# A block of feed-forward, attention and feed-forward on one core: maxima of the first half of tokens beside the first Q and K, ranking behind the next maxima, dot products behind the statistics

## The reference, cut to what matters

```python
# x: 8 samples x 1024 tokens x 512
def ffn(x):                       # capacity 0.75: the 768 tokens with the largest scores
    scores = x @ w_router
    top = top_k(scores, 768)
    return x with gelu(x[top] @ w_block) at the places top
def attn(x):                      # 16 heads of 32, latents of 64, causal
    Q = x @ Wq.T
    lk, lv = x @ Wk_down.T, x @ Wv_down.T
    q_lat = einsum('bthd,hdl->bthl', Q, q_to_latent)
    attn = softmax(causal(q_lat @ lk.T / 8))
    heads = einsum('bthl,hld->bthd', attn @ lv, v_up)
    return heads @ Wout.T
x = x + 0.5 * ffn(layernorm(x))   # first feed-forward, s = 0, f = 0
x = x + attn(layernorm(x))        # attention, s = 1
x = x + 0.5 * ffn(layernorm(x))   # second feed-forward, s = 2, f = 1
```

## Time and profile before

| | |
|---|---|
| median of 3 runs | 2528.2 us (2514.88 to 2531.42) |
| the profiled execution's own time | 2527.03 us |
| its span | 2525.3 us |
| PE busy | 2256.9 us, 89% |
| DVE busy | 1805.5 us, 71% |
| ACT busy | 1179.3 us, 47% |
| POOL busy | 396.6 us, 16% |
| mean granted clock of PE | 0.957 |

### The profile page before, as it was taken

The page is one execution under the profiler, slowest core; times in us unless marked ns, Lnnn a source line. Parts: engine busy times, 40 slices in busy tenths (PEclk is TensorE's granted clock), DMA queues, the critical chain, the costliest instruction groups (busy, mean ns, idle before and its releaser), DMA issues.

```text
span 2525.3 us, 53119 instructions
## 1 busy us (share of the span) xinstructions
PE 2256.9 (89%) x21504; PEld 1399.1 (55%) x21504; DVE 1805.5 (71%) x5077; ACT 1179.3 (47%) x2070; POOL 396.6 (16%) x510
## 2 busy tenths in 40 slices
PE   5769999899889998899998999989998899988976
PEld 4534477445664556644675446654476445664445
DVE  5658748887677766787667875788757787677726
ACT  3325643465424654356534564445543465424442
POOL 0101111112101121111211102111211112101121
PEclk9869999999998999999998999999999899998998
DMA  3200021100201002010111102210021100301000
GB/s 129 100 1 3 2 84 51 68 2 15 87 35 68 2 18 84 34 69 3 39 62 54 49 2 68 68 68 3 2 92 43 68 2 2 101 1 68 2 2 34
DMA packets 69601, 106.42 MB, mean 42 GB/s; under 512 B 2544, under 2 KB 32752, under 8 KB 67312
## 3 DMA queue, kind: packets, MB, share of 16 engines
q1 hardware_dynamic: 69360, 103.03, 12.0%
HBM read 64.75 MB, written 37.75 MB: 41 GB/s over the span
## 4 chain that ended last, share of the span: by engine, by line
PE 66%; DVE 14%; issue 11%; ACT 7%; POOL 2%; DMA 0%; DVEq 0%; POOLq 0%; ACTq 0%
PE psum L726 22%; PE psum L739 18%; PE psum L839 9%; PE psum L846 7%; PE psum L742 4%; DVE psum L984 4%; ACT pr L706 4%; PE psum L768 2%; PE psum L753 2%; DVE part L982 2%; POOL rstd L599 1%; DVE junk L934 1%; DVE junk L917 1%; DVE nt_l L907 1%; ACT nt_h L625 1%
## 5 line engine op out<-in xcount | busy, mean ns | idle before, releaser
L706 ACT ACTIVATE pr<-psum 128x512 f32<-128x512 f32 x1152 | 617.8, 596 | 629.6 <-PE psum L742 629.5
L739 PE MATMUL psum<-qk,qk 32*128 32x512 f32 (+3 forms) x4608 | 515.3, 370 | 118.2 <-ACT pr L706 40.0
L984 DVE CUSTOM_DVE_ANT_0 psum<-psum,mask_b 128x512 f32<-128x512 f32 (+3 forms) x1024 | 472.9, 522 | 127.9 <-PE psum L753 126.4
L739 PEld LDWEIGHTS psum<-qk,qk 32*128 32x128 f32 x4608 | 323.0, 187 | 419.5 <-ACT pr L706 117.6
L753 PE MATMUL psum<-qk,qk 32*128 32x512 f32 (+3 forms) x4608 | 517.8, 375 | 29.2 <-DVE part L982 19.7
L982 DVE TENSOR_REDUCE part<-psum 128x1 f32<-128x512 f32 x512 | 325.1, 681 | 77.9 <-PE psum L753 76.4
L753 PEld LDWEIGHTS psum<-qk,qk 32*128 32x128 f32 x4608 | 314.8, 189 | 56.0 <-DVE part L982 26.2
L617 POOL TENSOR_SCALAR_AFFINE_SELECT pr<-pr 128x512 f32<-128x512 f32 x256 | 159.2, 640 | 1022.3 <-ACT pr L706 1022.3
L839 PE MATMUL psum<-pr,v_sb 128*32 128x512 f32 (+3 forms) x3072 | 312.4, 502 | 1.6 <-ACT ht L625 1.6
L846 PE MATMUL psum<-pr,ones 128*32 128x512 f32 (+3 forms) x3072 | 306.0, 493 | 0.0
L646 ACT ACTIVATE norm<-x,nmr,rstd 128x512 f32<-128x512 f32 x192 | 152.3, 810 | 202.4 <-DVE nmr L901 202.4
(11 more groups left out here) (109 smaller groups left out, 3291.3 us busy)
## 6 DMA issues: line engine op xcount, KB each, us to landing
x<-x_dram SPq DMA_DIRECT2D x16, 1024.0 KB, 6.8
spill_x<-x SPq DMA_DIRECT2D x16, 1024.0 KB, 4.7
x<-spill_x SPq DMA_DIRECT2D x16, 1024.0 KB, 6.4
out_dram<-x SPq DMA_DIRECT2D x16, 1024.0 KB, 4.3
w_h<-scratch_o SPq DMA_DIRECT2D x28, 256.0 KB, 3.1
w_l<-scratch_o SPq DMA_DIRECT2D x28, 256.0 KB, 3.4
w_h<-scratch_q SPq DMA_DIRECT2D x6, 1024.0 KB, 4.9
w_l<-scratch_q SPq DMA_DIRECT2D x6, 1024.0 KB, 7.0
```

The lines of the kernel that those rows point to most:

```text
L706: nc.scalar.activation(pr_of(b, g, u)[:, 2 * p + place, :], bank(e, place), ACT.Exp, scale=SCALE).then_inc(exp_ready, 1)
L739: eng.matmul(o, (k_h, k_h, k_l)[t][own, P * j:P * (j + 1)], (q_h, q_l, q_h)[t][own, queries], start=(t == 0 and at == 0), stop=False, skip ...
L984: m = nc.vector.tensor_tensor_reduce(scores, scores, mask_b[:, BANK - w:BANK], 1.0, FAR, ALU.add, ALU.max, top_of)
```

## The change

Nothing is computed in another way and each engine has the same work (`MC` gets a wait for all maxima of its half, because the last unit of the list is no longer the last one made). The order of the list changes in four places, and with it the banks that the rings give:

1. In `project`, Q 1 and K 0 of the first half now follow Q 0 directly, maxima units 7 and 8 (which need only the first half of Q and K) come beside T 6 and T 7, before the second LAT; they take their banks from ring H. The K and V of the second half are put in another order among Q, maxima and HS.
2. In `back`, units 7 and 8 are gone, MC 0 and XT 0 come directly with MC 1 and XT 1, the variance of the second half comes before the dot products, and all dot products come after all statistics.
3. Of the eight ranking parts, 0 and 1 stay in `back`; 2 to 7 go into the first four pairs of the next attention group, behind the maxima there. RF, GX, CB, the store and the next load follow three pairs later. In the last sample there is no next attention, and they stay in `back`.
4. At the start, after `project(0)`, only units 5 and 6 remain.

```diff
@@ -147,18 +147,18 @@
         for i in range(TC):
             out += [("T", 1, b, i)] + ([("NO", 1, b, i + 2)] if i + 2 < TC else []) + (left[i] if left else []) + after[i]
         out += [("LAT", b, 0), ("XS", b, 0), ("NO", 1, b, 4), ("NO", 1, b, 5)]
-        out += [("Q", b, 0, 0), ("T", 1, b, 4), ("NO", 1, b, 6)]
-        out += [("Q", b, 1, 0), ("T", 1, b, 5), ("NO", 1, b, 7), ("T", 1, b, 6)]
-        out += [("Q", b, 2, 0), ("T", 1, b, 7), ("Q", b, 3, 0), ("LAT", b, 1), ("XS", b, 1)]
+        out += [("Q", b, 0, 0), ("Q", b, 1, 0), ("K", b, 0, 0), ("T", 1, b, 4), ("NO", 1, b, 6)]
+        out += [("Q", b, 2, 0), ("T", 1, b, 5), ("NO", 1, b, 7), ("T", 1, b, 6)] + maxima(b, 0, 7)
+        out += [("Q", b, 3, 0), ("T", 1, b, 7)] + maxima(b, 0, 8) + [("LAT", b, 1), ("XS", b, 1)]
         out += [("XR", b - 1, 0), ("XR", b - 1, 1)] if b else [("XL", 1, 0), ("XL", 1, 1)]
         splits = [[("HS", b - 1, g, c)] if b else [] for c in range(NC) for g in range(NQ)]
-        keys = [[("K", b, n // NC, n % NC), ("V", b, n)] for n in range(NT)]
+        keys = [[("K", b, n // NC, n % NC)] for n in range(NT)]
         loads = [[("W2", b - 1, "o", g)] if b else [] for g in range(NQ)]
-        out += keys[0] + splits[0] + keys[1] + splits[1] + [("Q", b, 0, 1)] + loads[0]
-        out += keys[2] + splits[2] + [("Q", b, 1, 1)] + loads[1] + maxima(b, 0, 0) + splits[3]
-        out += [("Q", b, 2, 1)] + loads[2] + maxima(b, 0, 1) + keys[3] + [("Q", b, 3, 1)] + loads[3] + maxima(b, 0, 2)
-        out += keys[4] + splits[4] + keys[5] + splits[5] + maxima(b, 0, 3)
-        out += keys[6] + splits[6] + keys[7] + splits[7] + maxima(b, 0, 4)
+        out += [("Q", b, 0, 1)] + loads[0] + keys[1] + [("V", b, 0)] + splits[0] + [("V", b, 1)] + splits[1]
+        out += [("Q", b, 1, 1)] + loads[1] + maxima(b, 0, 0) + splits[2] + [("Q", b, 2, 1)] + loads[2] + maxima(b, 0, 1) + splits[3]
+        out += keys[2] + [("V", b, 2), ("Q", b, 3, 1)] + loads[3] + maxima(b, 0, 2) + keys[3] + [("V", b, 3)] + splits[4]
+        out += keys[4] + [("V", b, 4)] + splits[5] + maxima(b, 0, 3) + keys[5] + [("V", b, 5)] + splits[6]
+        out += keys[6] + [("V", b, 6)] + splits[7] + maxima(b, 0, 4) + keys[7] + [("V", b, 7)]
         return out
 
     def maxima(b, g, u):
@@ -227,18 +227,16 @@
             return [("O", b, i)] + stats(2, b, i)
 
         out = added(0) + added(1) + more(maxima, 5) + added(2) + added(3) + scales(2, b, 0)
-        out += added(4) + [("NO", 2, b, 0), ("NO", 2, b, 1)] + more(maxima, 6) + dot(1, b, 0)
-        out += added(5) + turn(0) + dot(1, b, 1) + added(6) + more(gathered, 1) + turn(1) + dot(1, b, 2)
-        out += added(7) + turn(2)[:1] + dot(1, b, 3) + more(turned, 1)
+        out += added(4) + [("NO", 2, b, 0), ("NO", 2, b, 1)] + more(maxima, 6) + added(5) + turn(0)
+        out += added(6) + more(gathered, 1) + turn(1) + added(7) + more(gathered, 0) + more(turned, 1)
+        out += [("VA", 2, b, 1), ("RS", 2, b, 1)] + turn(2)[:1] + dot(1, b, 0) + [("NM", 2, b, 1)] + more(turned, 0)
         out += ([("W2", b + 2, "q", 0)] if b + 2 < B else [])
-        out += layer(1, b, 0) + turn(3)[:1] + scales(2, b, 1) + [("NO", 2, b, 4), ("NO", 2, b, 5)]
-        out += layer(1, b, 1) + turn(4) + turn(5) + [("SC", 1, b, 0)] + dot(1, b, 4) + more(maxima, 7) + turn(6) + turn(7)
-        out += dot(1, b, 5) + dot(1, b, 6) + layer(1, b, 2) + dot(1, b, 7) + more(maxima, 8) + layer(1, b, 3)
-        out += [("SC", 1, b, 1)] + more(gathered, 0)
-        out += layer(1, b, 4) + [("RT", 1, b, 0), ("RT", 1, b, 1)] + more(turned, 0)
-        out += layer(1, b, 5) + [("RT", 1, b, i) for i in range(2, NT)]
+        out += layer(1, b, 0) + turn(3)[:1] + [("NO", 2, b, 4), ("NO", 2, b, 5)] + dot(1, b, 1) + dot(1, b, 2)
+        out += layer(1, b, 1) + turn(4) + dot(1, b, 3) + turn(5) + dot(1, b, 4) + turn(6) + [("SC", 1, b, 0)] + turn(7) + dot(1, b, 5)
+        out += layer(1, b, 2) + dot(1, b, 6) + dot(1, b, 7) + layer(1, b, 3) + [("SC", 1, b, 1)]
+        out += layer(1, b, 4) + [("RT", 1, b, 0), ("RT", 1, b, 1)] + layer(1, b, 5)
         if b + 1 == B:
-            out += layer(1, b, 6) + layer(1, b, 7)
+            out += [("RT", 1, b, i) for i in range(2, NT)] + layer(1, b, 6) + layer(1, b, 7)
         return out
 
     def ending(b):
@@ -248,17 +246,19 @@
         return out
 
     sched = [("XL", 0, 0), ("XL", 0, 1)] + front(0) + project(0, None)
-    for u in range(5, UNITS):
-        sched += maxima(0, 0, u) + sum([gathered(0, 0, c) + turned(0, 0, c) for c in range(NC) if LAST[c] == u], [])
+    sched += maxima(0, 0, 5) + maxima(0, 0, 6) + sum([gathered(0, 0, c) + turned(0, 0, c) for c in (1, 0)], [])
     for b in range(B):
         groups, left = attention(b)
         if b > 0:
 
-            groups[0][0] += [("F", 1, b - 1, 6)]
-            groups[0][1] += [("F", 1, b - 1, 7), ("G", 1, b - 1, 6), ("G", 1, b - 1, 7)]
+
+            groups[0][0] += [("F", 1, b - 1, 6), ("RT", 1, b - 1, 2), ("RT", 1, b - 1, 3)]
+            groups[0][1] += [("F", 1, b - 1, 7), ("G", 1, b - 1, 6), ("G", 1, b - 1, 7), ("RT", 1, b - 1, 4), ("RT", 1, b - 1, 5)]
+            groups[0][2] += [("RT", 1, b - 1, 6)]
+            groups[0][3] += [("RT", 1, b - 1, 7)]
             tail = ending(b - 1)
             tail.append([("XL", b + 1, c) for c in range(NC)] if b + 1 < B else [("XR", b, c) for c in range(NC)])
-            groups[0] = [weave(groups[0], tail, 0, len(groups[0]) // 2)]
+            groups[0] = [weave(groups[0], tail, 3, len(groups[0]) // 2 + 3)]
         if b + 1 < B:
             ahead = [[e] for c in range(NC) for i in range(TC * c, TC * (c + 1))
                      for e in stats(0, b + 1, i) + (scales(0, b + 1, c) if i % TC == TC - 1 else [])]
@@ -321,7 +321,7 @@
         if e in beside_of:
             continue
         if k in ("S", "MX"):
-            early = k == "MX" and e[2] == 0 and e[3] <= 4
+            early = k == "MX" and e[2] == 0 and e[3] not in (5, 6)
             own = take("H", 0, 8, 4) if early else take("N", 0, 4, 4) if k == beside[e][0] else take("A", 0, 6, 4)
             banks[e], banks[beside[e]] = own[1::2], own[0::2]
         elif k == "XT":
@@ -986,7 +986,8 @@
                         m.then_inc(mx_free, 1)
                 elif k == "MC":
                     b, g, c = e[1:]
-                    dve.wait_ge(mx_free, 2 * max(nth["MX", b, g, LAST[c], p] for p in range(2)))
+                    dve.wait_ge(mx_free, 2 * max(nth["MX", b, g, u, p] for u in range(UNITS) for p in range(2)
+                                                 if any(i // TC == c for i, n in MAXIMA[u])))
                     if c:
                         nc.vector.tensor_reduce(mx[:, 1, :, :], part[:, :, TC:NT, :], AX_X, ALU.max).then_inc(max_ready, 1)
                     else:
```

## The result

| | before | after |
|---|---|---|
| median | 2527.7 us (4 runs) | 2491.1 us (4 runs, 2485.7 to 2492.3) |
| ratio, with its 95% interval | 1 | 0.9865 [0.984, 0.9889] |
| the profiled execution, its span | 2527.03, 2525.3 us | 2491.35, 2489.6 us |
| mean granted clock of PE | 0.957 | 0.963 |

The change makes the kernel faster by 1.35%, or 36 us. That is in the range, but the forecast was a gain of 65: 29 us are missing, more than a measurement's doubt.

What follows compares the result with a forecast made beforehand. PE, busy 89%, was taken as bound by its waits and clock, chiefly pair 2 waiting for DVE's ranking. Seven changes with 2 us for sample 4 give -52.2, first sample -7, last -5.5: 2527.0 - 64.7 = 2462 us, 8-in-10 range 2438 to 2500.

Steps and rivals of the forecast that it cites:

- (a): Beside Q and K: maxima units 7 and 8 move here; first output projection 1.4 us later per change.
- (b): The back: PE loses 1.98 us of maxima and a 1.47 wait, gains waits of 1.1, 1.3, 0.8; net -0.3.
- the 2 us for sample 4: First output projection: sample 4 newly waits for its bank behind the last maxima; 2 us charged once.
- (c): Start of attention, s being pair 1's start: pair 7 at s+20.5 instead of s+29.69; -9.2 us per change.
- (d): Behind the start of attention, per change: later additions and load +0.3 us, a slow stretch after the first wait +0.75.
- (e): First sample: two of four maxima units move away from before its first pair; -7 us, between -11 and -3.
- (f): Last sample: a 2.7 wait for normalised tiles and slow matmuls go, ranking starts earlier; -5.5 us, between -3 and -7.
- the two small waits: In the back, behind transpose 6: waits for scores and tile 7, 0.8 us more per change.
- A: Rival, chance 0.18: clock falls at the first new wait and stays low, or latent 1 is fully delayed; 2487 us.
- B: Rival, chance 0.05: brief, frequent waits keep the clock low through the attention group; slower, 2582 us.
- low for one stretch at most: Sign for (d): the clock is 1.0 on expert tile 7 and low in one stretch at most.
- D: Rival, chance 0.10: the back's 1.1 and 1.3 waits do not appear and pairs 4 to 6 wait less; 2443 us.

Runs made afterwards that it cites:

- gx_spread: gx_early with ranking parts 2 to 7 cut into their instructions and spread over seven pairs, chain and next statistics later; 2455.58 us, ratio 0.9738.
- gx_early: The changed kernel with all eight scalings queued on POOL directly behind the finish of the ranking; 2458.97 us, ratio 0.9739.
- rank_only: The kernel before with only ranking parts 2 to 7 and the woven chain moved; 2497.67 us, ratio 0.9898.

## Why the prediction was right, and where not

The sum, term by term, against what the stages measured (us, all seven changes together unless said):

| term of the prediction | forecast | measured |
|---|---|---|
| (a), (b): up to pair 1, with the 2 us for sample 4 | +4.8 | -4.5 |
| (c): pair 1 to 7 | -64.4 | -54.6 |
| (d): one slow stretch | +5.3 | 0: it lies in pair 5 and 6, within the -54.6 |
| (d): the moved chain, behind pair 7 | +2.1 | +32.8 |
| (e): first sample | -7 | -6.1 |
| (f): end | -5.5 | -2.7 |
| other groups | 0 | -0.5 |
| sum | -64.7 | -35.7 |

**(d) failed: the moved chain was put at 0.3 us a change and cost 4.7, in all 31 us more.** The step read "The additions and the load of the sample after next come three chunks later and reach pairs whose maxima come in narrower pieces on DVE: +0.3". It costed the moved chain on the engine that was at issue, DVE, and not on the engine that feeds it. The scalings move too, and they are POOL's. Walking POOL's queue, as DVE's was walked, would have found the wait, though not its price: the first mask stands behind pair 10 in the list, and in the new order three of the eight scalings come behind it. The earlier trace rows named POOL as the one that the additions wait for: 2.7 us in the whole kernel, which became 26.9. The Trainium skill, page "PSUM — Partial Sum Buffer", section "Engine vs sequencer instructions", has the rule in a clause: the queues of ScalarE, VectorE and GpSimdE are strict first-in, first-out. By that rule a GX behind an AM waits for the exponentials that the AM waits for; this case's trace agrees (8.39 us with the scaling's operands ready).

**(c): the mechanism and the new value were right, the old value was not.** The forecast said pair 7 at s+20.5 and waits of about 2 at pairs 4 to 6. After has 20.35 to 20.71, pair 2 and 3 at s+4.07 and s+8.14 (forecast 4.0, 8.0) and these waits:

```profile
1349.14 0.49 PE L739 MATMUL psum<-qk,qk 32*128 32x512 f32 x2 [1.69 <-DVE part L982]
...
1351.94 0.79 PE L739 MATMUL psum<-qk,qk 32*128 32x512 f32 x2 [1.61 <-DVE part L982]
...
1353.94 1.94 PE L839 MATMUL psum<-pr,v_sb 128*32 128x512 f32 x8
...
1355.81 0.79 PE L739 MATMUL psum<-qk,qk 32*128 32x512 f32 x2
```

The wait of pair 6 is not there: the clock falls at pair 5 (0.79 for 0.49), its step takes 3.87, and the slow PE covers what DVE is late. But "today pair 7 is at s+29.69" took the one sample that I had cut as typical. It was the slowest of the seven: 26.62, 29.18, 26.26, 29.69, 27.33, 29.63 and 29.58, mean 28.3. That is 9.6 of the 9.8 us by which this term is off. I had read the 6.6 to 7.0 us of waiting in all seven changes, but not the stage; in samples 1 and 3 the second slow stretch doesn't come at all, in 5 it comes and the first is shorter (5.7 us from pair 2 to 3, elsewhere 6.4 to 7.1).

**(a) and (b): the single waits came as forecast, the side effects were better.** The rows at their places in after, latent 1 (0.8 forecast), the first output projection (a wait for sample 4), the transpose of maxima (1.1) and transpose 6 (1.3):

```profile
1260.15 0.47 PE L726 MATMUL psum<-nt_h,wlat_h 128*128 128x512 f32 x1 [0.71 <-DVE nt_l L907]
...
1289.63 0.50 PE L726 MATMUL psum<-w_h,nt_h 128*128 128x512 f32 x1 [1.23 <-DVE part L984]
...
1316.63 0.28 PE L829 MATMUL psum<-ident,mx 128*16 128x128 f32 x1 [1.04 <-DVE mx L994]
...
1324.84 0.63 PE L768 MATMUL psum<-ident,norm 128*128 128x128 f32 x4 [1.09 <-DVE nt_l L907]
1325.73 0.62 PE L774 MATMUL psum<-ident,scol 128*128 128x128 f32 x4 [0.26 <-DVE scol L924]
```

The stage up to the output projection grows by 13.7, where 1.4 a change and 2 for sample 4 make 11.8. The back shrinks by 2.6 a change. Here the prediction has a slip: its own waits and the 1.98 add up to the "net -0.3" that it states, but the sum takes -1.98 + 0.8, which is -1.2. With -0.3 the first pair would stand at 1351.6, 1.1 later than before and not 0.4, and the forecast at about 2467. (As it stands, 1350.45 + 1.4 - 1.98 + 0.8 is 1350.67, 0.2 later.)

Two things made the back better than either figure. "With 0.8 more for the two small waits" was 0.26, and a wait of 0.30 for a low half that before had there went as well; in samples 4 and 5, where the clock is 1.00 in both kernels, the back is 1.8 shorter. And a wait at the output projection can cost the clock behind it: in before the back takes 52.95 in sample 2, with the 2.79 wait ahead of it and clock 0.95, and 50.28 in sample 4 at 1.00; in after, waits of 2.43 and 1.23 are followed by 50.05 and 48.48. It does not always: after has the wait of 1.89 twice, followed by 50.01 at clock 0.97 in sample 3 and by 48.44 at 1.00 in sample 7. The differences between the kernels in this stage are 1.8 to 4.6 us a change, and the four largest (2.9, 2.1, 3.1, 4.6) are where before had this wait (samples 2, 3, 6 and 7).

**(e), (f).** The first sample gave 6.1 of 7. At the end the wait of 2.74 for a normalised tile went as forecast, but a wait of 1.05 for a low half, the same as at 1324.84, came in its place; I had priced it in the seven changes and left it out of the last.

**The rivals.** A said 2487, 4 us from what was measured, and for another reason: it had the clock fall at the first wait and pair 7 at s+25; pair 7 came at s+20.5 and the clock held through both expert tiles; nor was latent 1 late by the full DVE time (0.71). The right time for the wrong cause, which only the stage table tells. B (2582) needed slow steps beyond pair 8: there are none in pair 7 to 11 (8.48 at 1.00). But the lower level did come once more, behind waits of 1.6 us between pairs 11 and 15 (0.75 in the window shown). So of the Trainium skill's page "TensorE: Matmul & The Clock Gate", section "A second HAM failure mode: psum-queue depth-cycling", the trace agrees with the oscillation between two levels under short waits for banks, and shows that here it ended each time within a few pairs; the loss stays at one to three slow steps. The sign "low for one stretch at most" was not met: there are two. D fell with the waits of 1.04 and 1.09 in the back.

## What to carry to other kernels

When a chain is moved, walk the queue of every engine that issues a part of it, also of one that is 16% busy: an in-order queue makes an idle engine late as soon as something that waits stands ahead of something that is ready. Issue what is ready ahead of what must wait, at the point where it becomes ready (here all eight scalings at once); this costs nothing where it doesn't matter and was worth 32 us where it did. And take a stage's old value from all its repeats, not from the one that was looked at in detail.

## What the runs showed of the hardware

**The same waits, two clocks.** In gx_spread the waits of 1.56 and 0.78 us ahead of pairs 4 and 5 were followed by 0.50 in six sample changes and by 1.00 in one, with equal instructions; in four of the seven, three slow and the fast one, all pairs up to pair 5 even start at the same times (s+4.07, 8.15, 10.9, 12.88). A slow stretch there costs 2.7 us. In before the same stage took 26.3 to 27.3 three times and 29.2 to 29.7 four times. What decides it has not been found, so a forecast can give such a stretch only a chance.

**A short wait can cost more than itself.** In after, pair 11 to 15 of the sample shown runs at clock 0.75 behind the wait of 1.64 at 1371.28. Against gx_early's 9.22 it takes 4.4 us more: 1.4 of it is idle time of PE (1.63 against 0.27), and 3.1 is slow matmuls (12.02 us busy against 8.95 for 148 and 149 of them). The same queue can cost waits alone. In rank_only, sample change 1 to 2, the clock stays at 1.00 in this stage, with waits of 1.63 and 1.94 at pairs 12 and 14:

```profile
775.73:788.32 12.59, 9.03 (x152) 5.05 (x148) 8.72 (x36) 4.39 (x9) 4.12 (x6) 1.00 0.21 74
```

**An addition beside POOL's work takes longer.** A 128x512 addition of line 955 takes 0.74 us (0.735 to 0.753, 36 times in after) and, beside an instruction of POOL, up to 1.18 (28 times, mean 1.07).
